# One Mamba-and-attention kernel on one core: softplus for two channel tiles at a time, and the slots of a chunk dealt again

## What is computed

```python
xn = layernorm(groupnorm(x)) * ln_w + ln_b
xb, z = split(xn @ in_proj_w.T)              # 768 channels each
xc = silu(conv4_causal(xb) + conv_b)
dt, Bm, Cm = split(xc @ x_proj_w.T)          # 24, 16 and 16 columns
dt = softplus(dt @ dt_w.T + dt_b)            # 768 channels
h[t] = exp(dt[t] * A) * h[t-1] + (dt[t] * xc[t]) * Bm[t]    # 16 states a channel
y = (h * Cm).sum(states) + xc * D
x = x + (y * silu(z)) @ out_proj_w.T
```

## Time and profile before

| | |
|---|---|
| median of three runs | 6579.67 us |
| the profiled execution | 6579.83 us |
| its span, first to last instruction | 6577.7 us |
| of that the scan, first to last gate | 142.0 to 5358.4 us |
| mean granted TensorE clock | 0.967 of full speed |
| busy share, TensorE / VectorE / ScalarE / GpSimd | 92 / 90 / 76 / 78% |
| ScalarE's table loads for softplus | 2 x 192, 1283 ns each |

### The profile page before, as it was taken

How to read it: one execution, slowest core, us unless ns; L and a number is a source line. 1 busy time by engine, 2 the same in 40 slices (tenths; PEclk the granted TensorE clock), 3 DMA queues, 4 the chain that set the end, 5 groups by cost and what they waited for, 6 DMA issues and landing times. The chain is left out here.

```text
span 6577.7 us, 105792 instructions
## 1 busy us (share of the span) xinstructions
PE 6067.4 (92%) x35452; PEld 3884.7 (59%) x35452; DVE 5924.9 (90%) x7357; ACT 5010.0 (76%) x10458; POOL 5105.1 (78%) x4137
## 2 busy tenths in 40 slices
PE   7999999999999999999999999999999869999998
PEld 3555555555555555555555555555555557777776
DVE  6999999999999999999999999999999976666666
ACT  3888888888888888888888888888888854343443
POOL 2999999999999999999999999999999961010100
PEclk8999999999999999999999999999999989999999
DMA  6222222222222222222222222222222312222222
GB/s 262 102 100 100 100 100 100 100 100 100 100 101 100 101 100 100 100 100 102 102 101 100 100 100 100 100 100 100 100 100 100 119 43 71 84 84 81 91 74 72
DMA packets 175235, 656.80 MB, mean 100 GB/s; under 512 B 28044, under 2 KB 28268, under 8 KB 149860
## 3 DMA queue, kind: packets, MB, share of 16 engines
q1 hardware_dynamic: 174692, 650.05, 26.9%
HBM read 477.19 MB, written 153.88 MB: 96 GB/s over the span
## 5 line engine op out<-in xcount | busy, mean ns | idle before, releaser
L967 POOL TENSOR_TENSOR dbx<-u,bb 128x512 f32<-128x512 f32 x3072 | 3836.1, 1276 | 261.5 <-DVE h L811 210.4
L801 DVE TENSOR_TENSOR_SCAN p_da<-p_da,state_v,dbx 128x512 f32<-128x512 f32 x1728 | 2165.3, 1274 | 0.8 <-ACT p_da L627 0.6
L627 ACT ACTIVATE p_da<-dt,neg_a 128x512 f32<-128x512 f32 x3072 | 2091.0, 692 | 72.5 <-DVE h L811 27.0
L811 DVE TENSOR_TENSOR_SCAN h<-p_da,state_h,dbx 128x512 f32<-128x512 f32 x1344 | 1703.8, 1275 | 138.1 <-ACT p_da L627 106.4
L1108 PEld LDWEIGHTS p_yt<-ident,hc_v 128*128 128x128 f32 x6912 | 872.0, 146 | 803.4 <-issue 644.8
L820 DVE TENSOR_TENSOR hc_v<-cc,p_da 128x512 f32<-128x512 f32 x1728 | 1144.5, 672 | 24.0 <-PE p_yt L1108 20.4
L1037 PE MATMUL p_g<-xs,win 128*128 128x512 f32 x2304 | 1155.6, 599 | 3.8 <-DVE xs L770 3.4
L1108 PE MATMUL p_yt<-ident,hc_v 128*128 128x128 f32 x6912 | 1074.7, 283 | 87.0 <-DVE hc_v L820 85.4
L976 POOL TENSOR_TENSOR hc_g<-h,cc 128x512 f32<-128x512 f32 x768 | 978.2, 1274 | 0.0
L1033 PE MATMUL p_g<-xb,cdiag 128*128 128x512 f32 x1536 | 766.0, 595 | 1.9 <-ACT halo L573 1.9
L661 ACT ACTIVATE hct<-p_yt,ct 128x128 f32<-128x128 f32 x2304 | 655.7, 373 | 44.5 <-PE p_yt L1147 44.5
(11 more groups left out here) (163 smaller groups left out, 8580.0 us busy)
## 6 DMA issues: line engine op xcount, KB each, us to landing
bb<-bc_spill SPq DMA_DIRECT2D x128, 1024.0 KB, 10.1
cc<-bc_spill SPq DMA_DIRECT2D x64, 1024.0 KB, 8.0
xc_spill<-xc SPq DMA_DIRECT2D x96, 512.0 KB, 2.6
z_spill<-zt SPq DMA_DIRECT2D x96, 512.0 KB, 3.9
xj<-xc_spill SPq DMA_DIRECT2D x192, 256.0 KB, 4.1
zj<-z_spill SPq DMA_DIRECT2D x192, 256.0 KB, 2.7
cc<-x SPq DMA_DIRECT2D x48, 768.0 KB, 5.9
xc<-in_x SPq DMA_DIRECT2D x33, 768.0 KB, 10.7
```

The lines of the kernel that those rows point to most:

```text
L627: nc.scalar.activation(p_da[n % RD][:], dt[:, d % 2, :], ACT.Exp, scale=neg_a[:, d, n:n + 1])\
L801: nc.vector.tensor_tensor_scan(psum, psum, dbx[:, n % RB, :], state_v[:, d, k:k + 1], ALU.mult, ALU.add).then_inc(s_scan, 1)
L811: nc.vector.tensor_tensor_scan(h[:, k, :], psum, dbx[:, n % RB, :], state_h[:, d, k:k + 1], ALU.mult, ALU.add).then_inc(s_scan, 1)
L967: nc.gpsimd.tensor_tensor(dbx[:, n % RB, :], u[:, d % 2, :], bb[:, n, :], ALU.mult)\
```

## The change

- `softplus_pair` runs in odd tiles at step 7 and makes dt for the next two tiles. The first projection is copied from PSUM into its row of dt (a Copy, which any table set holds), so that the bank is free for the second; then come the table load, softplus in place in SBUF, softplus of the second projection out of PSUM, and the load back. Before the first chunk the pair for tiles 0 and 1 is made.
- Both projections go to p_yt[0]: `project_dt` at TensorE's steps 6 and 7 of odd tiles, the second behind the copy (semaphore s_dtr). In odd tiles that is the bank in which y is turned back and the states are turned; `turn_state` there waits for both softplus, and in even tiles for the gate. `add_skip` follows.
- dt has three rows instead of two, indexed d % 3.
- The slots are dealt anew, as the diff's first part shows. The silus move to steps 47, 64 and 80. The copies out of the projection banks stand one step behind their last matmul, and their last one is at 78 (before: 77). GpSimd's C products come 3 steps behind their state instead of 4, TensorE adds them 1 step behind instead of 6; turned states go at (9, 12, 14) and (10, 13, 15) instead of (8, 9, 13) and (8, 12, 14).

```diff
--- before.py
+++ after.py
@@ -51,19 +51,20 @@
 
 RB, RH, RD = 4, NHS, 4
 RV, RG = 3, 3
-TURN_STATE_AT, TIMES_CT_AT, KEEP_AT = (8, 9, 13), (8, 12, 14), 13
-LAG, LAG_V, LAG_G = 4, 2, 6
+TURN_STATE_AT, TIMES_CT_AT, KEEP_AT = (9, 12, 14), (10, 13, 15), 13
+LAG, LAG_V, LAG_G = 3, 2, 1
 OUT_BANK = (1, 1, 0)
 
-MEAN_AT, CENTRE_AT, SQUARE_AT = 4, (4, 7, 10), (3, 7, 9)
-VAR_AT, RSTD_AT, NORM_AT = 11, 10, (14, 15, 17)
-OUT_AT, OUT_SLOTS, RESIDUAL_AT = (7, 12, 18), (4, 4, 3), (11, 17, 24)
-IN_AT, IN_SLOTS = (22, 41, 59), (18, 18, 19)
-COPY_LATER, SILU_LATER = 0, (9, 6, 3)
-X_AT, COPY_X_AT, TURN_C_AT, COPY_CT_AT, SCALE_AT = (78, 80, 81), 82, 85, 86, (88, 89, 93)
-
-COPY_Y_AT, TURN_AT, GATE_AT = 1, 5, 6
-DT_AT, SOFTPLUS_AT, DT_X_AT = 6, 6, 12
+MEAN_AT, CENTRE_AT, SQUARE_AT = 2, (4, 8, 10), (5, 8, 9)
+VAR_AT, RSTD_AT, NORM_AT = 11, 11, (15, 16, 17)
+OUT_AT, OUT_SLOTS, RESIDUAL_AT = (6, 13, 19), (3, 3, 1), (13, 18, 25)
+IN_AT, IN_SLOTS = (22, 40, 60), (18, 18, 18)
+COPY_LATER, SILU_LATER = 1, (7, 6, 2)
+X_AT, COPY_X_AT, TURN_C_AT, COPY_CT_AT, SCALE_AT = (78, 79, 81), 84, 85, 89, (91, 94, 95)
+
+COPY_Y_AT, TURN_AT, GATE_AT = 1, 4, 6
+DT_AT, SOFTPLUS_AT, DT_X_AT = 6, 7, 15
+DT_NEXT_AT = 7
 
 
 def out_at(j, t):
@@ -274,7 +275,7 @@
         squares = [zt[:, 0, :], zt[:, 1, :], xb[:, 0, 0:CH]]
         xd = sb("xd", [64, CH])
 
-        dt = sb("dt", [P, 2, CH])
+        dt = sb("dt", [P, 3, CH])
         u = sb("u", [P, 2, CH])
         xj = sb("xj", [P, CH])
         zj = sb("zj", [P, CH])
@@ -330,6 +331,7 @@
         s_u = sem("u_done")
         s_dtm = sem("dt_mm")
         s_dt = sem("dt_done")
+        s_dtr = sem("dt_taken")
         s_xju = sem("skip_added")
         s_yts = sem("yt_copied")
         s_yb = sem("yb_done")
@@ -598,13 +600,19 @@
                 act.wait_ge(s_dtm, q * ND)
                 nc.scalar.activation(xd[:], p_g[1][0:64, :], ACT.Copy).then_inc(s_xd, 1)
 
-            def softplus(i, d):
+            def softplus_pair(i, d):
 
                 m = i * ND + d
                 act.wait_ge(s_dtm, m + 1)
                 act.wait_ge(s_exp, m * NS)
                 act.wait_ge(s_u, m)
-                nc.scalar.activation(dt[:, d % 2, :], p_yt[d % 2][:], ACT.Softplus, bias=dtb[:, d:d + 1]).then_inc(s_dt, 1)
+                nc.scalar.activation(dt[:, d % 3, :], p_yt[0][:], ACT.Copy).then_inc(s_dtr, 1)
+                act.preload_act_table_set("softplus")
+                act.wait_ge(s_dtr, m // 2 + 1)
+                nc.scalar.activation(dt[:, d % 3, :], dt[:, d % 3, :], ACT.Softplus, bias=dtb[:, d:d + 1]).then_inc(s_dt, 1)
+                act.wait_ge(s_dtm, m + 2)
+                nc.scalar.activation(dt[:, (d + 1) % 3, :], p_yt[0][:], ACT.Softplus, bias=dtb[:, d + 1:d + 2])\
+                    .then_inc(s_dt, 1)
                 act.preload_act_table_set(EXP_LN)
 
             def copy_y(i, d):
@@ -624,7 +632,7 @@
                     act.wait_ge(s_stv, m * NDV + BY_DVE.index(before) + 1 - (NDV if n < RD else 0) + C_STV)
                 else:
                     act.wait_ge(s_scan, m * NS + n - RD + 1 + C_SCAN)
-                nc.scalar.activation(p_da[n % RD][:], dt[:, d % 2, :], ACT.Exp, scale=neg_a[:, d, n:n + 1])\
+                nc.scalar.activation(p_da[n % RD][:], dt[:, d % 3, :], ACT.Exp, scale=neg_a[:, d, n:n + 1])\
                     .then_inc(s_exp, 1)
 
             def pack_heads():
@@ -691,7 +699,7 @@
                     silu(0, k // 6)
             copy_xd(0)
             copy_ct(0)
-            softplus(0, 0)
+            softplus_pair(0, 0)
             for n in range(RD):
                 decay(0, 0, n)
             for j in range(NJ):
@@ -718,8 +726,8 @@
                             pack_heads()
                         if n == COPY_Y_AT:
                             copy_y(i, d)
-                        if n == SOFTPLUS_AT and after[0] < NCH:
-                            softplus(*after)
+                        if n == SOFTPLUS_AT and d % 2 and after[0] < NCH:
+                            softplus_pair(*after)
                         g = d * NS + n
                         if g in SCALE_AT and q + 1 < NCH:
                             scale(q + 1, SCALE_AT.index(g))
@@ -955,7 +963,7 @@
                 pool.wait_ge(s_dt, m + 1)
                 pool.wait_ge(s_xjl, m * 16 + 16)
                 pool.wait_ge(s_dbx, m * NS)
-                nc.gpsimd.tensor_tensor(u[:, r, :], dt[:, r, :], xj[:], ALU.mult).then_inc(s_u, 1)
+                nc.gpsimd.tensor_tensor(u[:, r, :], dt[:, d % 3, :], xj[:], ALU.mult).then_inc(s_u, 1)
 
             def times_b(i, d, n):
                 m = i * ND + d
@@ -1052,8 +1060,11 @@
                 m = i * ND + d
                 if d == 0:
                     pe.wait_ge(s_xd, i + 1)
-                pe.wait_ge(s_gate, m + C_ONE)
-                nc.tensor.matmul(p_yt[d % 2][:], wdt[:, d * P:(d + 1) * P], xd[0:RANK, :], start=True, stop=True)\
+                if d % 2 == 0:
+                    pe.wait_ge(s_gate, m + C_ONE)
+                else:
+                    pe.wait_ge(s_dtr, m // 2 + 1)
+                nc.tensor.matmul(p_yt[0][:], wdt[:, d * P:(d + 1) * P], xd[0:RANK, :], start=True, stop=True)\
                     .then_inc(s_dtm, 1)
 
             def out_step(i, j, t):
@@ -1087,7 +1098,10 @@
 
                 m = i * ND + d
                 pe.wait_ge(s_xjl, m * 16 + 16)
-                pe.wait_ge(s_dt, m + 1)
+                if d % 2 == 0:
+                    pe.wait_ge(s_dt, m + 2)
+                else:
+                    pe.wait_ge(s_gate, m + C_ONE)
                 pe.wait_ge(s_ht, m * NTN + NTN)
                 for b in range(NT):
                     last = nc.tensor.matmul(p_yt[d % 2][:, b * P:(b + 1) * P], xj[:, b * P:(b + 1) * P], ddiag[:, d, :],
@@ -1138,8 +1152,8 @@
 
                 m, k = i * ND + d, BY_TURN.index(n)
                 pe.wait_ge(s_scan, m * NS + n + 1 + C_SCAN)
-                if m + 1 < NCH * ND:
-                    pe.wait_ge(s_dt, m + 2)
+                if d % 2 == 1 and m + 1 < NCH * ND:
+                    pe.wait_ge(s_dt, m + 3)
                 else:
                     pe.wait_ge(s_gate, m + 1 + C_ONE)
                 pe.wait_ge(s_ht, m * NTN + k + NTN)
@@ -1177,6 +1191,7 @@
                 project_x(0, third)
             turn_c(0)
             project_dt(0, 0)
+            project_dt(0, 1)
 
             def body(i, kind, b):
                 if kind == "image":
@@ -1188,8 +1203,10 @@
                         g = d * NS + n
                         if n == TURN_AT:
                             turn_back(i, d)
-                        if n == DT_AT and (d < ND - 1 or q < NCH):
+                        if n == DT_AT and d % 2 and (d < ND - 1 or q < NCH):
                             project_dt(*((i, d + 1) if d < ND - 1 else (q, 0)))
+                        if n == DT_NEXT_AT and d % 2 and (d < ND - 1 or q < NCH):
+                            project_dt(*((i, d + 2) if d < ND - 1 else (q, 1)))
                         for j in range(NJ):
                             for t in range(ND):
                                 if g == out_at(j, t):
```

## The result

The changed kernel takes 6596.67 us (median of 11 runs, 6591.42 to 6601.81) against 6579.7 us (11 runs) of the kernel before: ratio 1.0025, 95% interval 1.0016 to 1.0034. It is **slower by 0.25%**, 17 us. The time lies inside the forecast range of 6500 to 6615 us, but the direction is not the one forecast (6565 us, faster). All comparisons are between executions in the fast state; one of the five executions of in23_48_71 took 15304.87 us and is left out of its ratio, though not of its median. The profiled execution's span is 6594.9 us against 6577.7.

What follows compares the result with a forecast made beforehand. VectorE's own work, about 157.5 us a chunk, was taken as the floor, the rest as waiting. Terms summed to -0.5 us a chunk over 31 chunks (-15.5), plus 1.3 at the start: about -14, 6565 us, range 6500 to 6615.

Steps and rivals of the forecast that it cites:

- ScalarE's savings: Softplus on ScalarE: a pair takes 4.5 us instead of 6.5, saving 2.0 us a pair, 6.1 a chunk.
- Silu 1, +0.3: First silu, moved from step 48 to 47: VectorE's wait becomes 1.3 to 1.4 us instead of 1.13; +0.3 a chunk.
- Pair at 55, +0.2: Softplus pair at step 55: decays 12 and 14 come 0.2 us late each at worst; +0.2 a chunk.
- Silu 2, -0.25: Second silu, step 64: first late decay costs 1.15 us instead of 2.30, copies add 0.9; -0.25 a chunk.
- Silu 3, +0.4: Third silu, step 80: decay 5 is 1.2 us late where 0.8 is lost now; +0.4 a chunk.
- Mean, gate, residual, -1.15: Earlier slots: gate's 0.4 and first residual's 0.3 us go, the mean's wait falls by 0.45 a chunk.
- Second projection, cost 0: TensorE's second dt projection in odd tiles is covered before its softplus needs it; cost taken 0.
- The third rival: Second softplus waits 1 us for TensorE behind in-steps; 1 us instead of 2 saved, 6575 us; chance 0.08.
- GpSimd's lead, no cost: GpSimd's lead at step 10 falls to about 1 us, enough while VectorE waits behind the silus.
- The start: Before the first scan the copy and the second softplus are exposed; +1.3 us.
- The second rival: times_ct ahead of the silus waits for TensorE's turned state, landing on VectorE; 6611 to 6648 us; chance 0.25.
- 0.32 for "slower": Whole kernel: chance 0.32 of slower, against 0.46 faster and 0.22 same.

Runs made afterwards that it cites:

- in23_48_71: Changed kernel with the first input-projection step at 23 instead of 22, the first silu at step 48 and the second at 71; 6630.67 us.
- after_silu48: Changed kernel with the first silu at step 48 instead of 47; 6603.04 us, ratio 1.0039.
- pair_old_slots: Changed kernel keeping the softplus pair but with the slot constants of the kernel before; 6703.52 us, ratio 1.0194.
- silu47_71: Changed kernel with only the second silu moved, from step 64 to 71; 6591.92 us, ratio 1.0023.
- before_mean: Kernel before with only the new slots of mean, centring, squares, output projection, residual, normalising and turning back y; 6713.02 us, ratio 1.0209.
- single_new_slots: Kernel before with all the new slots, but one softplus a tile (step 7) and two rows of dt; 6607.91 us, ratio 1.0047.

## Why the prediction was wrong

**ScalarE's savings.** Right: 2.0 us a pair (197 us over 96 pairs), no drain at a table load. The Trainium skill (ScalarE: Activation LUTs, "What ACT_TABLE_LOAD costs") has 2.66 us a switch, drain included. Neither kernel shows more than 1.28 for a load, and the instructions on either side of it follow within 0.02 us (2181.75 + 0.72 and 2182.49, 2182.49 + 1.28 and 2183.78). By that page the pair would save an estimated 4.8 us, where the prediction has 4.7.

**Silu 1, +0.3; measured +1.1 in its wait, +0.99 in the tile.** This is the step that failed. The sum for decay 4 started at the end of VectorE's last product, as if ScalarE were there at once ("ScalarE is on time by then anyway"), and its 1.4 was then set against a measured 1.13 that has ScalarE's lateness in it. The lateness stood in the trace of the kernel before, where ScalarE keeps the last state at

```profile
2013.59 0.19 ACT L644 ACTIVATE state_v<-p_da 128x1 f32<-128x1 f32 x1
```

while the product had ended at 2012.46: 1.13 us late. The changed kernel is 1.03 late at the same place, and 1.0 + 1.3 is, within 0.1, the 2.25 that was measured. What differs is what is still to come. In the kernel before, one times_ct (step 14) stands behind step 13, and it is already part of the lateness; then come decays 3 and 4 and the silu. In the changed kernel two stand there (13 and 15): the first, with the halo copy of step 45, makes the lateness, and the second comes on top, 1.0 us. With the silu at the same step 48 the waits are 1.13 (before) and 1.81 (after_silu48), so 0.7 of the 1.1 us comes with the slots and the other 0.4 with the silu's move to 47. The pair has no part in it (pair_old_slots: 1.13).

**Pair at 55, +0.2; measured +0.57.** The same lateness, passed on. after_silu48 and in23_48_71 bear it out: a quarter of a microsecond taken at silu 1 comes back here.

**Silu 2, -0.25 in the forecast.** The two waits measured 1.36 and 0.84 in every chunk (1.15 and 0.9 forecast), 2.20 against 2.31 before: -0.1. Right in mechanism, copy_y and the copy at 65 between two decays; short by 0.15. silu47_71 shows that these waits belong to step 64.

**Silu 3, +0.4; measured +0.24.** The size of the wait came out (1.18 us, forecast 1.2; 0.66 in the kernel before), but it is VectorE's wait for TensorE to free hc_v, as in the kernel before, and not for a late decay 5.

**Mean, gate, residual, -1.15.** Measured -0.74, -0.20 and -0.35, together -1.3. The mean's wait went wholly and not by half; the gate's -0.48 was partly lost to the next point. The first residual's wait was one of low clock: in the kernel before tile 0 takes 30.25 us in 16 chunks at a granted clock of 1.00 and 31.0 in 15 at 0.94, and in the changed kernel 30.26 in all. before_mean shows that these gains hang on other slots of the change, which I had not seen.

**Second projection, cost 0.** Wrong in a few chunks (3 of 12 between 1500 and 3500 us, six of 31 in all). ScalarE's rows and then TensorE's in such a chunk:

```profile
2800.43 0.72 ACT L612 ACTIVATE dt<-dt,dtb 128x512 f32<-128x512 f32 x1
2802.93 0.69 ACT L614 ACTIVATE dt<-p_yt,dtb 128x512 f32<-128x512 f32 x1 [1.78 <-PE p_yt L1067]
```

```profile
2797.78 2.98 PE L1045 MATMUL p_g<-xs,win 128*128 128x512 f32 x4
...
2801.54 1.35 PE L1067 MATMUL p_yt<-xd,wdt 24*128 24x512 f32 x2
```

The softplus waits 1.78 us; in a chunk at full clock it waits 0.14. Two in-steps (four records) ahead of the second projection take 2.98 us here, where they take 1.98 us in a chunk at full clock (from 2962.85); the granted clock was 0.64 in these 2.98 us. With the product and the projection behind them TensorE comes 1.64 us later, which is the difference of the two waits. The third rival had the mechanism and 1 us as price for every pair; it cost 1.45 us in six chunks of 31, some 9 of the 17 us (an estimate: 6 x 1.45). Of the costs that the sum left out, only those at silu 1 and at 55 are larger.

**GpSimd's lead, no cost.** Right where VectorE waits elsewhere. In the last chunk, without those waits, it decides; VectorE's timeline:

```profile
5332.55 1.29 DVE L809 TENSOR_TENSOR_SCAN p_da<-p_da,state_v,dbx 128x512 f32<-128x512 f32 x1 [0.19 <-issue]
...
5335.00 1.29 DVE L809 TENSOR_TENSOR_SCAN p_da<-p_da,state_v,dbx 128x512 f32<-128x512 f32 x1 [0.58 <-issue]
```

The profile names no releaser ("issue"). GpSimd's timeline has the dbx that these scans read:

```profile
5331.19 1.28 POOL L975 TENSOR_TENSOR dbx<-u,bb 128x512 f32<-128x512 f32 x1
5332.41 1.27 POOL L984 TENSOR_TENSOR hc_g<-h,cc 128x512 f32<-128x512 f32 x1
5333.63 7.42 POOL L975 TENSOR_TENSOR dbx<-u,bb 128x512 f32<-128x512 f32 x6
```

The first dbx ends at 5332.47, and the first of the next six, by their mean of 1.24, at 5334.87: each 0.1 us ahead of a scan that waited. Such waits come to 1.5 us in this chunk and to 1.7 in single_new_slots, both with LAG = 3, and there are none in the kernel before and in pair_old_slots, both with LAG = 4; no run changed LAG alone. With gate waits of 0.4 to 0.8 the chunk is 2.3 us longer, which the forecast had left out. The start was not 1.3 us longer but 0.7 shorter.

**Rivals.** The second rival (slower by ScalarE's lateness at the silus) had the right place and sign but another mechanism: ScalarE hardly waited for TensorE's turned states there (L669 is not among its waits), it was simply full. 0.32 for "slower" was too low for a sum of -14 us in which the terms at the silus rested on one assumption about who is on time.

What stays open: which of the new slots the pair needs, what LAG alone is worth, and why the low clock falls on tile 1 in six chunks of the changed kernel, in 23 of silu47_71 and in none of the kernel before.

## What to carry to other kernels

Where engines walk one hand-dealt schedule, don't start the sum for a moved block at the moment the neighbour releases it: add up the engine's own work over the steps ahead and see whether it gets there on time; and don't set a sum that leaves its lateness out against a measured wait that has it in. A long block costs more than its cover: look at what stands behind it on its engine and frees a buffer for an engine without room. And gains read at several slots are not terms to be added until one knows which other slots they need.

## What had not been expected of the hardware

TensorE's granted clock decided more than one of the comparisons, and not only in tile 5, where TensorE has idle time (18.44 us busy of 25.74), but in tile 1 as well, where it is busy nearly throughout (25.35 of 26.07). In tile 5 it was 0.93 instead of 0.81 and the mean took 2.74 us instead of 4.06. In six chunks of 31 a stretch at the low level fell on tile 1 (0.64 over 3 us), and 1.64 us more for TensorE's steps became a wait of 1.78 us on ScalarE. The changed kernel so has chunks of 163.55 and of 165.04 us. The same tile at the same clock takes the same time to within 0.1 us in both kernels compared (26.07 at 1.00, 27.5 at 0.94 in the changed kernel and in silu47_71): what a slot costs is read from tiles at equal clock, and how often the low level comes is counted apart.
